# A column-gated layer's token sort with bf16 one-hots, weights placed later, gathers 12 tiles ahead and more unread matrix products

## The chip, the cores and the metric

The kernel runs on one core of a Trainium2 chip. A core has five engines that run their own instruction streams and wait for each other by semaphores: TensorE (PE in the profile; PEld is its loading of the stationary operand), VectorE (DVE), ScalarE (ACT), GpSimd (POOL) and SyncE (SP). Here SyncE and GpSimd issue the DMAs. TensorE's clock has two levels, 1.2 and 2.4 GHz; the profile shows what was granted as a share of 2.4 GHz. The metric is the device time of one execution in microseconds, as the median of several.

## The reference, cut to what matters

Four layers follow each other on 32 batches of 112 tokens with 256 features. Three of them (a depooling layer, a generated feed-forward layer and an attention layer) are not touched. The last one sends every token through one of 16 columns:

```python
def _L1_ffn_ref(x, col_emb, gate_w1, gate_b1, gate_w2, gate_b2, W_cols, b_cols, proj_w, proj_b, ln_g, ln_b):
    similarity = jnp.einsum('bsd,cd->bsc', _l2norm(x), _l2norm(col_emb))
    h = jax.nn.gelu(x @ gate_w1 + gate_b1, approximate=False)
    logits = similarity + jax.nn.sigmoid(h @ gate_w2 + gate_b2)
    _, top_idx = jax.lax.top_k(logits, 1)                   # one column of 16 for each token
    mask = jnp.sum(jax.nn.one_hot(top_idx, 16), axis=-2)
    weights = mask * jax.nn.softmax(logits, axis=-1)
    cols = jax.nn.gelu(jnp.einsum('bsd,cdn->bscn', x, W_cols) + b_cols, approximate=False)
    y = (cols * weights[..., None]).reshape(Bq, Sq, -1) @ proj_w + proj_b + x
    mu, var = jnp.mean(y, -1, keepdims=True), jnp.var(y, -1, keepdims=True)
    return (y - mu) * jax.lax.rsqrt(var + 1e-05) * ln_g + ln_b

x = x + jnp.tanh(g_ffn[1]) * _L1_ffn_ref(_layernorm(x), ...)
```

Since the mask leaves one column per token, only that column's product (256 to 64 features and back to 256) has to be computed.

## The kernel before

The kernel has a stage for each layer; the change is in `stage4` (from line 1497), the last one. It has two halves.

**Scoring and sort.** For groups of four batches TensorE turns the normalised tokens, computes the gate's products and the similarities, and ScalarE and VectorE make logits. VectorE then marks each token's best column (`hit`), counts along batches (`cum`), and TensorE's three products (lines 1987 to 1989) give each token's rank in its column. From the rank VectorE computes a slot. Slots are laid out by column in sub-tiles of 64, two to a tile of 128, 36 tiles in all (`N_TILES`), so a tile holds tokens of at most two columns. To invert the map, VectorE writes `in_tile` (which of 36 tiles, a one-hot, line 1856), `carry` (that one-hot times the token's number plus one, and times its weight, line 1861) and `spot` (which of 128 rows in the tile, in four quarters of eight batches, line 1865), all f32. TensorE multiplies `spot` of each of the 32 batches by `carry` and accumulates (line 1997): the result has, for each row and tile, the token's number and its weight. From it VectorE makes `comes_from`, `weight` and `goes_to` (lines 1870 to 1873) and then the columns of the 72 sub-tiles, `column_of` (lines 1875 to 1878).

Between these steps TensorE runs products that nobody reads: `busy(count, cols)` (line 1981) multiplies bf16 ones by a bf16 mask of 512 columns, or of `cols`, into PSUM bank 7.

**The tile loop.** For each of 36 tiles SyncE loads `column_of` twice into a register and issues two weight loads into a ring of four (lines 1633, 1634). GpSimd gathers the tile's rows by an indirect DMA (`fetch`, line 1666) and scatters finished rows (`store`, line 1674); its stream is written as `AHEAD4` = 5 gathers first, then for each n a gather n + 5 and the stores that are due after tile n. The first store is due after n = 5, so 11 gathers stand ahead of it. TensorE's stream for tile n is: `turn(n+1)` (two 128-column transposes, line 2006), `column(n)` (four products, 2017), `output(n-1)` (two register loads, 2022, and two products, 2026), and one unread product of 256 columns. ScalarE evacuates the turned rows (1725) and applies the gelu (1735), with a square root for every group of four tiles (1742). VectorE adds, takes statistics and finishes rows two tiles or more behind (1883 to 1910).

Every order here is written out by hand: each engine runs its list as it stands, and the waits between engines are semaphore counts. The unread products stand in TensorE's list, in front of what comes after them.

Of the kernel before, what the change touches and what calls it, by code (L numbers as in the profile page):

```python
# [19 lines left out]
ALU = mybir.AluOpType  # L20
# [3 lines left out]
BF16 = mybir.dt.bfloat16  # L24
I32 = mybir.dt.int32

B, T, D = 32, 112, 256
S2, DC = 375, 512
P = 128
# [892 lines left out]
def stage4_inputs(w):  # L922

    sb = lambda n, s, d=F32: w.ctx.enter_context(w.nc.sbuf_tensor(n, s, d))
    w.columns = {"col_emb": sb("s4_col_emb", [C4, D]), "cgate1": sb("s4_cgate1", [P, KD, P]),
                 "cgate1_b": sb("s4_cgate1_b", [P, 1]), "cgate2": sb("s4_cgate2", [P, C4]),
                 "cgate2_b": sb("s4_cgate2_b", [T, C4]), "w_cols": sb("s4_w_cols", [P, C4, KD * N4]),
                 "b_cols": sb("s4_b_cols", [N4, C4]), "proj": sb("s4_proj", [N4, F4 // N4 * D]),
                 "proj_b": sb("s4_proj_b", [T, D]), "proj_b_c": sb("s4_proj_b_c", [P, KD]),
                 "ln_g": sb("s4_ln_g", [P, D]), "ln_b": sb("s4_ln_b", [T, D]),  # L930
                 "col_less": sb("s4_col_less", [P, C4]), "steps": sb("s4_steps", [P, P + 1]),
                 "token": sb("s4_token", [T, B])}
    w.columns_in = w.sem("columns_in")
# [568 lines left out]
def stage4(w):  # L1502
# [6 lines left out]
    N_TILES, AHEAD4, SQRT_LAG = SLOT_TILES, 5, 2  # L1509
# [5 lines left out]
    with ExitStack() as ctx:  # L1515
# [30 lines left out]
        in_tile = sb("s4_in_tile", [T, B, N_TILES])  # L1546
        carry = sb("s4_carry", [T, B, 2, N_TILES])
        spot = sb("s4_spot", [T, B, P])
        pad = sb("s4_pad", [P, N_TILES])
        goes_to = sb("s4_goes_to", [P, N_TILES], I32)  # L1550
# [17 lines left out]
                 "counting", "cum_done", "rank_ps", "carry_done", "spot_done", "table_ps", "slots_done",  # L1568
# [12 lines left out]
        def wait(eng, name, count):  # L1581

            if count > 0:
                eng.wait_ge(S[name], count)
# [28 lines left out]
        with nc.Block() as block:  # L1613
# [26 lines left out]
            def _(pool):  # L1640
# [38 lines left out]
                wait(pool, "slots_done", 1)  # L1679
# [77 lines left out]
            def _(dve):  # L1757
# [102 lines left out]
                for part, of in enumerate((token, total)):  # L1860
                    nc.vector.tensor_tensor(carry[:, :, part, :], in_tile[:], of[:].unsqueeze(2).broadcast_to([T, B, N_TILES]),  # L1861
                                            ALU.mult).then_inc(S["carry_done"], 1)
                for q in range(4):
                    at = slice(q * 8, q * 8 + 8)
                    nc.vector.tensor_tensor(spot[:, at, :], steps[0:T, 0:P].unsqueeze(1).broadcast_to([T, 8, P]),
                                            within[:, at].unsqueeze(2).broadcast_to([T, 8, P]), ALU.is_equal)\
                        .then_inc(S["spot_done"], 1)
                wait(dve, "table_ps", 1)
                got = w.bank(1)[:, 2 * C4:2 * C4 + 2 * N_TILES].rearrange("p (k n) -> p k n", k=2)
                chain.link(nc.vector.tensor_scalar(pad[:], got[:, 0, :], 0.5, 65537.0, ALU.is_lt, ALU.mult))  # L1870
                nc.vector.tensor_scalar(comes_from[:], got[:, 0, :], -1.0, 0.0, ALU.add, ALU.max)
# [7 lines left out]
                wait(dve, "slots_done", 1)  # L1879
# [53 lines left out]
            def _(pe):  # L1933
# [51 lines left out]
                busy(24)  # L1985
# [6 lines left out]
                busy(36)  # L1992
                wait(pe, "carry_done", 2)
                for b in range(B):
                    if b % 8 == 0:
                        wait(pe, "spot_done", b // 8 + 1)
                    last = nc.tensor.matmul(w.bank(1)[:, 2 * C4:2 * C4 + 2 * N_TILES], spot[:, b, :],  # L1997
                                            carry[:, b, :, :].rearrange("t k n -> t (k n)"),
                                            start=(b == 0), stop=(b == B - 1))
                last.then_inc(S["table_ps"], 1)  # L2000

# [31 lines left out]
                turn(0)  # L2033
                for n in range(N_TILES):
# [5 lines left out]
                    busy(1, 256)  # L2040
# [3 lines left out]
def lay_out(x, ctx_2048, mask_BxS2_if0, g_xattn, g_ffn, L0_xattn_W_in, L0_xattn_b_in, L0_xattn_g_res,  # L2044
# [66 lines left out]
    out["token"] = (np.arange(B)[None] * T + np.arange(T)[:, None] + 1).astype(f32)  # L2111
# [14 lines left out]
```

## Time and profile before

| | us |
|---|---|
| median of 3 runs | 1323.33 (1322.43 to 1325.54) |
| the profiled execution, its own time | 1325.58 |
| its span, first to last instruction | 1323.6 |
| TensorE busy (matrix products) | 1227.8 (93%) |
| TensorE loading weights | 888.1 (67%) |
| VectorE busy | 958.7 (72%) |
| ScalarE busy | 676.3 (51%) |
| GpSimd busy | 583.4 (44%) |

The fourth stage runs from about 1080 us to the end: the scoring to about 1130, the sort to about 1168, the tile loop to about 1306.
### The profile page before, as it was taken

Reading aid. Unit: us, or ns where it says so; the run is one execution under the profiler, and the core shown is the slowest. Engines: PE = TensorE matmul, PEld = TensorE weight load, DVE = VectorE, ACT = ScalarE, POOL = GpSimd, SP = SyncE. Lnnn points to the kernel's source line nnn. Section 1 sums busy time; section 2 is a strip of 40 time slices with the busy share of each in tenths; the row PEclk is TensorE's granted clock in tenths of the full one; section 3 lists DMA queues with packets and bytes.
Section 4 is the critical chain, followed back from the end, with each engine's and each line's share of the span. In section 5 each row is a group of like instructions: output and inputs, shape, how many; then the busy total and the mean of one; then the engine's idle time right before and its main releaser. Section 6 shows DMA issues by size and latency. Waiting matters only on the chain. (4 is left out here: it accounts for less than half of the span.)

```text
span 1323.6 us, 33070 instructions
## 1 busy us (share of the span) xinstructions
PE 1227.8 (93%) x12491; PEld 888.1 (67%) x12491; DVE 958.7 (72%) x1666; ACT 676.3 (51%) x1497; POOL 583.4 (44%) x835
## 2 busy tenths in 40 slices
PE   4789999999999998699999999999999979889995
PEld 4565678778877885367667676767676657656663
DVE  7777665675576568788888888888888758624555
ACT  5845212202211222577888888788877653125442
POOL 1427888888875002633333333333333108034553
PEclk9999899999999999599999999999999988865555
DMA  8505445455453203976665666666666205243441
GB/s 222 144 4 192 139 132 166 137 152 154 146 154 97 72 1 50 159 114 96 97 99 95 96 95 95 96 95 95 95 95 95 37 1 160 64 124 108 141 134 38
DMA packets 111752, 141.80 MB, mean 107 GB/s; under 512 B 10317, under 2 KB 94776, under 8 KB 109380
## 3 DMA queue, kind: packets, MB, share of 16 engines
q1 hardware_dynamic: 97796, 96.14, 36.9%
q0 software_dynamic: 13824, 43.84, 11.3%
q8 instruction: 89, 1.46, 0.5%
q14 instruction: 43, 0.35, 0.1%
HBM read 105.79 MB, written 30.49 MB: 103 GB/s over the span
## 5 line engine op out<-in xcount | busy, mean ns | idle before, releaser
L1269 DVE TENSOR_REDUCE s_neg_max<-banks 112x3 bf16<-112x1461 f32 (+1 forms) x192 | 290.3, 1512 | 45.5 <-PE banks L1385 45.3
L1183 ACT ACTIVATE s_prob<-banks 128x448 f32<-128x448 f32 x512 | 272.6, 545 | 92.2 <-PE banks L1411 77.2
L714 DVE TENSOR_TENSOR s_m<-banks,s_base 128x512 f32<-128x512 f32 x256 | 161.1, 682 | 99.7 <-PE banks L868 99.4
L1411 PE MATMUL banks<-s_q_t,s_k_t 112*128 112x112 bf16 x2048 | 186.7, 215 | 1.1 <-ACT s_prob L1183 1.0
L1411 PEld LDWEIGHTS banks<-s_q_t,s_k_t 112*128 112x128 bf16 x2048 | 124.4, 98 | 72.7 <-issue 50.9
L868 PE MATMUL banks<-s_gate_sel,s_tw 64*128 64x256 f32 x1024 | 131.3, 396 | 1.2 <-DVE s_m L714 1.0
L911 PE MATMUL banks<-s_m,s_act_t 128*112 128x256 f32 x512 | 128.2, 388 | 1.5
L1427 PE MATMUL banks<-s_prob,s_v 128*32 128x112 f32 (+1 forms) x4096 | 126.3, 263 | 0.8 <-ACT s_prob L1183 0.7
L893 PEld LDWEIGHTS banks<-s_x_t,s_m 128*128 128x128 f32 x1024 | 116.7, 192 | 10.6 <-issue 7.6
L893 PE MATMUL banks<-s_x_t,s_m 128*128 128x112 f32 x1024 | 122.4, 278 | 0.0
L808 ACT ACT_TABLE_LOAD x8 | 10.3, 1283 | 205.3 <-PE banks L893 205.3
L868 PEld LDWEIGHTS banks<-s_gate_sel,s_tw 64*128 64x128 f32 x1024 | 95.2, 190 | 27.0 <-issue 9.7
L733 DVE SCALAR_TENSOR_TENSOR x_res<-banks,gates,x_res 112x512 f32<-112x512 f32 x128 | 93.0, 745 | 24.4 <-PE banks L911 21.0
L808 ACT ACTIVATE s_act_t<-banks,s_bias 128x112 f32<-128x112 f32 x256 | 68.9, 359 | 80.4 <-PE banks L893 80.3
L911 PEld LDWEIGHTS banks<-s_m,s_act_t 128*112 128x112 f32 x512 | 81.8, 176 | 38.7 <-issue 19.7
L1427 PEld LDWEIGHTS banks<-s_prob,s_v 128*32 128x32 f32 (+1 forms) x4096 | 94.9, 110 | 12.9 <-ACT s_prob L1183 1.0
L1067 POOL CAST s_qk<-s_rest 112x512 bf16<-112x512 f32 x32 | 19.6, 614 | 172.3 <-DVE s_rest L1258 172.3
L1057 POOL COPY s_v<-s_v_raw 128x768 f32<-128x768 f32 x32 | 26.3, 822 | 155.0 <-PE banks L1427 155.0
L1385 PE MATMUL banks<-s_k_t,s_q_t 32*112 32x487 bf16 x192 | 79.9, 416 | 5.7 <-DVE s_neg_max L1269 3.9
L1367 PE MATMUL banks<-s_ident,s_qk 112*128 112x112 bf16 x1024 | 73.4, 216 | 9.3 <-DVE s_q_t L1282 6.4
L1385 PE MATMUL banks<-s_k_t,s_q_odd 32*112 32x487 bf16 x320 | 80.4, 417 | 0.0
L2026 PE MATMUL banks<-s_proj,s_hid_c 64*128 x144 | 74.6, 671 | 0.7 <-ACT s_hid_c L1735 0.7
(304 smaller groups left out, 2284.7 us busy)
## 6 DMA issues: line engine op xcount, KB each, us to landing
k_parts<-s_k_split POOLq DMA_DIRECT2D x64, 281.2 KB, 3.5
s_k_t<-k_parts SPq DMA_DIRECT2D x32, 562.5 KB, 8.1
s_tw<-in_tw SPq DMA_DIRECT2D x16, 1024.0 KB, 5.1
s_k_raw<-in_ctx_k POOLq DMA_DIRECT2D x64, 187.5 KB, 3.6
s_k_t<-k_parts SPq DMA_DIRECT2D x32, 375.0 KB, 5.4
s_v_raw<-in_ctx SPq DMA_DIRECT2D x32, 256.0 KB
s_src<-in_ctx SPq DMA_DIRECT2D x8, 896.0 KB, 15.4
s_k_t<-k_parts SPq DMA_DIRECT2D x32, 187.5 KB, 9.2
```

The lines of the kernel that those rows point to most:

```text
L714: nc.vector.tensor_tensor(dst[:, :, :, rows_], got, base[:, :, rows_].unsqueeze(2).broadcast_to([P, 2, B, HR]), ALU.add).then_inc(S["merge ...
L733: nc.vector.scalar_tensor_tensor(out=w.x_res[:, 2 * p:2 * p + 2, :], in0=w.bank(6 + p % 2, T).rearrange("t (b d) -> t b d", b=2), scalar=w ...
L808: last = nc.scalar.activation(act_t[:, b, :], w.bank(4 + g % 2)[:, r * T:(r + 1) * T], ACT.Gelu_apprx_tanh, bias=bias1[:, c, b, :])
L868: last = nc.tensor.matmul(w.bank(2 * (n[1] % 2) + half)[:, m * B * HR:(m + 1) * B * HR], rows_(m)[tile], sel[tile], start=True, stop=True)
L893: last = nc.tensor.matmul(w.bank(4 + g % 2)[:, r * T:(r + 1) * T], m1[:, kk, b, :], x_t[:, kk, b * T:(b + 1) * T], start=(kk == 0), stop=( ...
L911: last = nc.tensor.matmul(y, act_t[:, b, :], m2[:, b, :], start=not first, stop=True)
L1183: nc.scalar.activation(prob[t % 2][:, c, :], w.bank(SCORE + n % SRING, P, TILE), ACT.Exp, scale=DH ** -0.5).then_inc(S["exp_done"], 1)
L1269: nc.vector.tensor_reduce(neg_max[half][:, ROWS + first:ROWS + end, 0], w.banks[0:T, MAX:MAX + end - first, 0:NKEY], AX.X, ALU.max, negate ...
L1385: last = nc.tensor.matmul(w.bank(MAX + place, T, NKEY), q, k_t[k][at, h, FIRST:FIRST + NKEY], start=True, stop=True)
L1411: last = nc.tensor.matmul(w.bank(SCORE + n % SRING)[:, s * T:(s + 1) * T], k_t[k][0:ROWS_MAX, h, c * P:(c + 1) * P], q_t[k][0:ROWS_MAX, h, :],
L1427: last = nc.tensor.matmul(w.banks[s * SLOT:(s + 1) * SLOT, OUT, t * T:(t + 1) * T], v[k][0:K_OF[c], c, t * HS + s, :], prob[t % 2][0:K_OF[ ...
L2026: last = nc.tensor.matmul(w.bank(4 + n % 3, P, D), hid_c[n % 2][:, k, :], proj[:, bass.ds(c * D, D)], start=(k == 0), stop=(k == 1))
```

## The change

The one-hots and carries become bf16, which a matrix product takes in one record instead of two. So that the token's number survives in bf16, it is carried in two parts, the batch (0 to 31) and the token in the batch plus one (1 to 112), and put together after the product (batch x 112 + token - 1). The weight is split into three bf16 parts and is placed by a product of its own, after the column numbers, into bank 6; `weight` is the sum of the three. The unread products of the sort are 32, 44, three pairs and 32 instead of 24, 36 and 16, and the tile loop runs two of 512 columns per tile instead of one of 256. TensorE waits for the weight placement ahead of `output(2)`, which writes bank 6. Gathers run 12 tiles ahead instead of 5. The diff, cut to its core:

```diff
@@ stage4
-    N_TILES, AHEAD4, SQRT_LAG = SLOT_TILES, 5, 2
+    N_TILES, AHEAD4, SQRT_LAG = SLOT_TILES, 12, 2
...
-        in_tile = sb("s4_in_tile", [T, B, N_TILES])
-        carry = sb("s4_carry", [T, B, 2, N_TILES])
-        spot = sb("s4_spot", [T, B, P])
+        in_tile = sb("s4_in_tile", [T, B, N_TILES], BF16)
+        carry = sb("s4_carry", [T, 5, B, N_TILES], BF16)
+        spot = sb("s4_spot", [T, B, P], BF16)
+        w_parts = sb("s4_w_parts", [T, 3, B], BF16)
+        rest = sb("s4_rest", [T, B])
...
@@ GpSimd
-                wait(pool, "slots_done", 1)
+                wait(pool, "slots_done", 2)
@@ VectorE
-                for part, of in enumerate((token, total)):
-                    nc.vector.tensor_tensor(carry[:, :, part, :], in_tile[:], of[:].unsqueeze(2).broadcast_to([T, B, N_TILES]),
-                                            ALU.mult).then_inc(S["carry_done"], 1)
+                nc.vector.tensor_scalar(carry[:, 0, :, :], in_tile[:], token[:, B:B + 1], None, ALU.mult)
+                nc.vector.tensor_tensor(carry[:, 1, :, :], in_tile[:], token[:, 0:B].unsqueeze(2).broadcast_to([T, B, N_TILES]),
+                                        ALU.mult).then_inc(S["carry_done"], 1)
...
+                chain.link(nc.vector.tensor_copy(w_parts[:, 0, :], total[:]))
+                chain.link(nc.vector.tensor_tensor(rest[:], total[:], w_parts[:, 0, :], ALU.subtract))
+                chain.link(nc.vector.tensor_copy(w_parts[:, 1, :], rest[:]))
+                chain.link(nc.vector.tensor_tensor(w_parts[:, 2, :], rest[:], w_parts[:, 1, :], ALU.subtract))
                 wait(dve, "table_ps", 1)
...
-                chain.link(nc.vector.tensor_scalar(pad[:], got[:, 0, :], 0.5, 65537.0, ALU.is_lt, ALU.mult))
-                nc.vector.tensor_scalar(comes_from[:], got[:, 0, :], -1.0, 0.0, ALU.add, ALU.max)
-                nc.vector.tensor_copy(weight[:], got[:, 1, :])
-                nc.vector.scalar_tensor_tensor(out=goes_to[:], in0=got[:, 0, :], scalar=-1.0, in1=pad[:],
-                                               op0=ALU.add, op1=ALU.add).then_inc(S["slots_done"], 1)
+                nc.vector.tensor_scalar(pad[:], got[:, 0, :], 0.5, 65537.0, ALU.is_lt, ALU.mult)
+                chain.link(nc.vector.tensor_scalar(found[:], got[:, 1, :], float(T), -1.0, ALU.mult, ALU.add))
+                chain.link(nc.vector.tensor_tensor(found[:], found[:], got[:, 0, :], ALU.add))
+                nc.vector.tensor_scalar(comes_from[:], found[:], 0.0, None, ALU.max).then_inc(S["slots_done"], 1)
+                nc.vector.tensor_tensor(goes_to[:], found[:], pad[:], ALU.add).then_inc(S["slots_done"], 1)
...
-                wait(dve, "slots_done", 1)
+                for part in range(3):
+                    nc.vector.tensor_tensor(carry[:, 2 + part, :, :], in_tile[:],
+                                            w_parts[:, part, :].unsqueeze(2).broadcast_to([T, B, N_TILES]), ALU.mult)\
+                        .then_inc(S["shares_done"], 1)
+                wait(dve, "shares_ps", 1)
+                got = w.bank(6, P, 3 * N_TILES).rearrange("p (k n) -> p k n", k=3)
+                chain.link(nc.vector.tensor_copy(weight[:], got[:, 2, :]))
+                for part in (1, 0):
+                    chain.link(nc.vector.tensor_tensor(weight[:], weight[:], got[:, part, :], ALU.add))
+                dve.sem_inc(S["weight_done"], 1)
@@ TensorE
-                busy(24)
+                busy(32)
...
-                busy(36)
-                wait(pe, "carry_done", 2)
+                busy(44)
+                wait(pe, "carry_done", 1)
                 for b in range(B):
                     if b % 8 == 0:
                         wait(pe, "spot_done", b // 8 + 1)
...
+                    last = placed(found_ps, slice(0, 2), b)
+                    if b % 8 == 7 and b < B - 1:
+                        busy(2)
                 last.then_inc(S["table_ps"], 1)
+                busy(32)
+                wait(pe, "shares_done", 3)
+                for b in range(B):
+                    last = placed(w.bank(6, P, 3 * N_TILES).rearrange("p (k n) -> p k n", k=3), slice(2, 5), b)
+                last.then_inc(S["shares_ps"], 1)
...
+                    if n == 2:
+                        wait(pe, "weight_done", 1)
...
-                wait(pe, "slots_done", 1)
-                busy(16)
                 wait(pe, "columns_done", 1)
+                wait(pe, "slots_done", 2)
...
-                    busy(1, 256)
+                    busy(2)
```

`placed(bank, parts, b)` is the product of `spot` of batch b with those parts of `carry`. Three places of the engines' lists show what moved.

TensorE, from the last unread products of the ranks to the first column products; `s_keep,s_ones` are the unread products, `s_carry,s_spot` the one-hot products, `ident,s_xn` the turns, `s_x_tt,s_w_tile` the column products. Before:

```order
L1981 MATMUL banks<-s_keep,s_ones 128x512 x36
L1997 MATMUL banks<-s_carry,s_spot 128x72 x32
L1981 MATMUL banks<-s_keep,s_ones 128x512 x16
L2006 MATMUL banks<-ident,s_xn 128x128 x4
L2017 MATMUL banks<-s_x_tt,s_w_tile 64x64 x4
L1981 MATMUL banks<-s_keep,s_ones 128x256
L2006 MATMUL banks<-ident,s_xn 128x128 x2
L2017 MATMUL banks<-s_x_tt,s_w_tile 64x64 x4
```

The same place after:

```order
L1997 MATMUL banks<-s_keep,s_ones 128x512 x44
L2010 MATMUL banks<-s_carry,s_spot 128x72 x8
L1997 MATMUL banks<-s_keep,s_ones 128x512 x2
L2010 MATMUL banks<-s_carry,s_spot 128x72 x8
...
L1997 MATMUL banks<-s_keep,s_ones 128x512 x32
L2010 MATMUL banks<-s_carry,s_spot 128x108 x32
L2033 MATMUL banks<-ident,s_xn 128x128 x4
L2044 MATMUL banks<-s_x_tt,s_w_tile 64x64 x4
L1997 MATMUL banks<-s_keep,s_ones 128x512 x2
L2033 MATMUL banks<-ident,s_xn 128x128 x2
L2044 MATMUL banks<-s_x_tt,s_w_tile 64x64 x4
```

The 32 one-hot products are cut into quarters with unread pairs between them, and a second set of 32 with 108 columns, behind 32 unread ones, stands ahead of the first turns.

VectorE, from the spot one-hots to the first row of the tile loop. Before:

```order
L1865 TENSOR_TENSOR s_spot<-s_steps,s_within 112x1024 x4
L1870 TENSOR_SCALAR s_pad<-banks 128x36
L1871 TENSOR_SCALAR s_comes_from<-banks 128x36
L1872 COPY s_weight<-banks 128x36
L1873 SCALAR_TENSOR_TENSOR s_goes_to<-banks,s_pad 128x36
L1875 TENSOR_TENSOR s_past<-s_steps,s_ends 1x1152
L1877 TENSOR_REDUCE s_column_f<-s_past 1x72
L1878 TENSOR_SCALAR s_column_of<-s_column_f 1x72
L1883 SCALAR_TENSOR_TENSOR s_xn<-banks,s_weight,s_xn 128x256
```

After, from the end of the weight's splitting:

```order
L1874 TENSOR_TENSOR s_w_parts<-s_rest,s_w_parts 112x32
L1877 TENSOR_SCALAR s_pad<-banks 128x36
L1878 TENSOR_SCALAR s_found<-banks 128x36
L1879 TENSOR_TENSOR s_found<-s_found,banks 128x36
L1880 TENSOR_SCALAR s_comes_from<-s_found 128x36
L1881 TENSOR_TENSOR s_goes_to<-s_found,s_pad 128x36
L1882 TENSOR_TENSOR s_past<-s_steps,s_ends 1x1152
L1884 TENSOR_REDUCE s_column_f<-s_past 1x72
L1885 TENSOR_SCALAR s_column_of<-s_column_f 1x72
L1887 TENSOR_TENSOR s_carry<-s_in_tile,s_w_parts 112x1152 x3
L1892 COPY s_weight<-banks 128x36
L1894 TENSOR_TENSOR s_weight<-s_weight,banks 128x36 x2
```

The weight's carry products and its sum now stand behind the column numbers, and four small operations (lines 1871 to 1874) stand ahead of the table.

GpSimd, the head of the tile loop. Before:

```order
L1666 DMA s_xn<-x_rows,s_comes_from 128x512 x11
L1674 DMA out_x<-s_xn,s_goes_to 3584x256
L1666 DMA s_xn<-x_rows,s_comes_from 128x512
L1674 DMA out_x<-s_xn,s_goes_to 3584x256
L1666 DMA s_xn<-x_rows,s_comes_from 128x512
```

After:

```order
L1669 DMA s_xn<-x_rows,s_comes_from 128x512 x16
L1669 DMA x_res<-x_rows,s_comes_from 128x512 x2
L1677 DMA out_x<-s_xn,s_goes_to 3584x256
L1669 DMA x_res<-x_rows,s_comes_from 128x512
L1677 DMA out_x<-s_xn,s_goes_to 3584x256
```

Eighteen gathers instead of eleven stand ahead of the first store; the ring's second half lies in the residual's buffer.

## Rows read from the trace of the kernel before

**Rows 1.** Stretches (us): length, busy time PE PEld DVE ACT POOL, clock, DMA share, GB/s.

```profile
1134.00:1138.00 4.00, 1.58 (x9) 0.59 (x7) 3.90 (x5) 1.61 (x3) 0.00 (x0) 1.00 0.00 1
1146.00:1149.50 3.50, 1.25 (x11) 1.13 (x11) 3.50 (x4) 0.00 (x0) 0.00 (x0) 1.00 0.00 0
1161.90:1166.60 4.70, 4.68 (x12) 1.66 (x13) 2.74 (x3) 0.00 (x0) 3.25 (x3) 0.50 0.30 76
1169.50:1173.50 4.00, 1.27 (x14) 1.02 (x15) 0.00 (x0) 1.02 (x4) 3.09 (x4) 1.00 0.88 260
...
1200.00:1220.00 20.00, 20.00 (x82) 13.24 (x82) 10.41 (x34) 8.79 (x25) 10.90 (x11) 0.50 0.46 133
```

**Rows 2.** Timeline, TensorE, sort and first tiles: start, us, what, [idle before <-releaser].

```profile
1138.22 7.93 PE L1981 MATMUL banks<-s_keep,s_ones 112*128 112x512 bf16 x36
1148.40 12.80 PE L1997 MATMUL banks<-s_carry,s_spot 112*128 112x72 f32 x64 [2.25 <-DVE s_spot L1865]
...
1170.65 0.65 PE L2017 MATMUL banks<-s_x_tt,s_w_tile 128*64 128x64 f32 x8 [2.12 <-DMA s_w_tile<-s_w_cols]
1171.23 0.28 PE L1981 MATMUL banks<-s_keep,s_ones 112*128 112x256 bf16 x1
1171.35 0.39 PE L2006 MATMUL banks<-ident,s_xn 128*128 128x128 f32 x2
...
1175.01 2.06 PE L2026 MATMUL banks<-s_proj,s_hid_c 64*128 x4 [0.75 <-ACT s_hid_c L1735]
```

**Rows 3.** Timeline, TensorE, one tile of the loop.

```profile
1199.81 0.39 PE L1981 MATMUL banks<-s_keep,s_ones 112*128 112x256 bf16 x1
...
1200.00 0.63 PE L2006 MATMUL banks<-ident,s_xn 128*128 128x128 f32 x2
...
1200.56 1.12 PE L2017 MATMUL banks<-s_x_tt,s_w_tile 128*64 128x64 f32 x8
...
1201.60 2.07 PE L2026 MATMUL banks<-s_proj,s_hid_c 64*128 x4
...
1203.61 0.39 PE L1981 MATMUL banks<-s_keep,s_ones 112*128 112x256 bf16 x1
```

**Rows 4.** Timeline, VectorE, the sort's one-hots and what follows the table.

```profile
1144.49 1.36 DVE L1861 TENSOR_TENSOR s_carry<-s_in_tile,s_token 112x1152 f32<-112x1152 f32 x1
...
1147.04 4.62 DVE L1865 TENSOR_TENSOR s_spot<-s_steps,s_within 112x1024 f32<-112x1024 f32 x4
1161.24 0.20 DVE L1870 TENSOR_SCALAR s_pad<-banks 128x36 f32<-128x36 f32 x1 [9.57 <-PE banks L1997]
...
1164.53 0.18 DVE L1878 TENSOR_SCALAR s_column_of<-s_column_f 1x72 int32<-1x72 f32 x1
```

**Rows 5.** Chain of waits at the loop's start: start, us, what it spent them on.

```profile
1168.20 0.49 SPq L1634
...
1169.38 3.81 DMA s_w_tile<-s_w_cols
```

**Rows 6.** Source view of the weight loads, line 1634, all 72.

```profile
DMA to landing us min/median/max: 1.8/1.9/4.3
```

**Rows 7.** Timeline, GpSimd, a store and the gather behind it.

```profile
1202.35 1.01 POOL L1674 DMA_INDIRECT out_x<-s_xn,s_goes_to  x1 [1.38 <-DVE s_xn L1910]
1203.66 0.98 POOL L1666 DMA_INDIRECT s_xn<-x_rows,s_comes_from  x1 [0.30 <-issue]
```

**Rows 8.** Timeline, TensorE, attention stage: eight bf16 products with 128 weight columns.

```profile
700.52 0.56 PE L1367 MATMUL banks<-s_ident,s_qk 112*128 112x112 bf16 x8
```

**Rows 9.** Timeline, ScalarE, evacuation of the first two turned tiles.

```profile
1168.20 1.14 ACT L1725 ACTIVATE s_x_tt<-banks,s_neg_b 128x128 f32<-128x128 f32 x4 [32.55 <-PE banks L2006]
```

**Rows 10.** Chain of waits, end of the loop and tail.

```profile
1302.80 1.05 PE banks L2017 x8
...
1305.89 0.48 DVE s_xn L1883
...
1315.84 1.58 POOLq L1613
```

More of the change, by code:

```diff
@@ L931, in stage4_inputs @@
                  "col_less": sb("s4_col_less", [P, C4]), "steps": sb("s4_steps", [P, P + 1]),
-                 "token": sb("s4_token", [T, B])}
+                 "token": sb("s4_token", [T, B + 1])}
     w.columns_in = w.sem("columns_in")
@@ L1545, in stage4 @@
         pos, tile_of, within = (sb("s4_" + n, [T, B]) for n in ("pos", "tile_of", "within"))
-        in_tile = sb("s4_in_tile", [T, B, N_TILES])
-        carry = sb("s4_carry", [T, B, 2, N_TILES])
-        spot = sb("s4_spot", [T, B, P])
+        in_tile = sb("s4_in_tile", [T, B, N_TILES], BF16)
[3 more added lines that the diff above has]
+        rest = sb("s4_rest", [T, B])
         pad = sb("s4_pad", [P, N_TILES])
+        found = sb("s4_found", [P, N_TILES])
         goes_to = sb("s4_goes_to", [P, N_TILES], I32)
@@ L1567, in stage4 @@
                  "col_ss_done", "col_n_done", "col_t_ps", "col_t_done", "biased", "kept", "x_biased", "kept_late", "x_biased_late",
-                 "counting", "cum_done", "rank_ps", "carry_done", "spot_done", "table_ps", "slots_done",
+                 "counting", "cum_done", "rank_ps", "carry_done", "spot_done", "table_ps", "slots_done", "shares_done", "shares_ps", "weight_done",
                  "columns_done", "turned", "x_tt_done", "col_ps", "gelu_done", "y_ps", "summed", "stat_done",
@@ L1990, in _, with placed @@
                                  stop=True).then_inc(S["rank_ps"], 1)
-                busy(36)
-                wait(pe, "carry_done", 2)
+                def placed(bank, parts, b):
+                    return nc.tensor.matmul(bank, spot[:, b, :], carry[:, parts, b, :],
+                                            start=(b == 0), stop=(b == B - 1))
+                busy(44)
+                wait(pe, "carry_done", 1)
+                found_ps = w.bank(1)[:, 2 * C4:2 * C4 + 2 * N_TILES].rearrange("p (k n) -> p k n", k=2)
                 for b in range(B):
@@ L1996, in _ @@
                         wait(pe, "spot_done", b // 8 + 1)
-                    last = nc.tensor.matmul(w.bank(1)[:, 2 * C4:2 * C4 + 2 * N_TILES], spot[:, b, :],
-                                            carry[:, b, :, :].rearrange("t k n -> t (k n)"),
-                                            start=(b == 0), stop=(b == B - 1))
+                    last = placed(found_ps, slice(0, 2), b)
+                    if b % 8 == 7 and b < B - 1:
+                        busy(2)
                 last.then_inc(S["table_ps"], 1)
+                busy(32)
[3 more added lines that the diff above has]
+                last.then_inc(S["shares_ps"], 1)
                 def turn(n):
@@ L2110, in lay_out @@
     out["steps"] = np.concatenate([np.tile(np.arange(P), (P, 1)), np.arange(P)[:, None]], 1).astype(f32)
-    out["token"] = (np.arange(B)[None] * T + np.arange(T)[:, None] + 1).astype(f32)
+    out["token"] = np.concatenate([np.tile(np.arange(B), (T, 1)), np.arange(T)[:, None] + 1], 1).astype(f32)
     return {k: np.ascontiguousarray(v) for k, v in out.items()}
```

## Prediction

> **What bounds the kernel now.** I read the slices of the page first: TensorE's granted clock reads 0.8 or 0.9 through most of the span and 0.5 in the last four, the part that the change rewrites. Then the stretches [rows 1], the timelines of TensorE, VectorE and GpSimd, the chain of waits and the weight-load line of the source view. The last stage ends in a loop over 36 gathered tiles. In it TensorE is busy for 20.00 of 20.00 us, at a granted clock of 0.50 (1.2 of 2.4 GHz), while VectorE has 10.41, ScalarE 8.79 and GpSimd 10.90 us [rows 1]. One tile takes 3.80 us from one unread product to the next, 1199.81 to 1203.61, and its parts fill it: unread product 0.19, two turns 0.56, column products 1.04, output products 2.01 [rows 3]. So the loop is bound by TensorE at its lower level.
>
> How it got there: ahead of the loop the 64 one-hot records take 12.80 us [rows 2], 0.20 each. They begin in a stretch in which TensorE was busy 1.25 of 3.50 us, behind which the clock fell. Sixteen unread products (4.68 of 4.70 us busy at 0.50) brought it back; then TensorE waited for weights, 1.27 of 4.00 us busy, and it fell for good. A stretch with 1.58 of 4.00 us busy did not lose it [rows 1]. The loop at 20.00 of 20.00 never got it back: busy time in a record is not what decides.
>
> **The sort.** VectorE's last quarter of the spot one-hots ends at 1147.04 + 4.62 = 1151.66, and the table is read at 1161.24 [rows 4]; in between stand the f32 products. With bf16 operands a product is one record. The nearest row is eight bf16 products with 128 weight columns in 0.56 us, 0.07 each [rows 8]. The last eight stand behind the last quarter, so the table is ready at about 1152.3: 8.9 us earlier. The four small operations that split the weight cost about 0.20 each, as the table's first row does [rows 4]; 0.8 us, of which those eight products hide 0.6. The decoding has one more dependent step of 0.2. Together -8.45 us: the column numbers, done at 1164.71 before (1164.53 + 0.18), are done at 1156.3. Bounds: the first of the two carry operations now has a per-partition scalar instead of a broadcast operand; it may cost the old 1.36 or a good deal less, so up to 1 us can be gained. The unread pairs between quarters (0.44) fit beside a quarter of 1.16.
>
> **The weights later.** Three carry products of 1.36 [rows 4] come behind the column numbers: 4.1 us, to 1160.4. The 32 unread products there (0.22 each, 7.93 / 36 [rows 2], 7.0 us) run from 1152.3 to 1159.3 and cover most of it, leaving about 1 us idle. Then 32 products of 108 columns, 0.07 each: 2.2 us, to 1162.6. The wait for shares_done has the gathered rows' turns queued behind it on TensorE. Two turns (0.39 for the pair [rows 2]) and the first evacuation (1.14 for two rows [rows 9]) put the first column product near 1163.7, against 1170.65: 7 us earlier. Its weights don't hold it: they land 5.9 us after the column numbers now (1164.71 to 1170.65), so at 1162.2. weight_done is due at about 1163.3, far ahead of the third output product that waits for it.
>
> The eight small products and the 32 are where a rule speaks against the trace. The row of eight gives 0.07 each [rows 8]. The Trainium skill, "TensorE: Matmul & The Clock Gate", LDWEIGHTS, states a load of P / 1.2 ns for P columns, 107 ns for 128; by that the 32 would take 3.4 us instead of 2.2 and the kernel would come out 1.2 us later. The same page's section on the weight path allows faster loads for bf16 with 128 columns, and the row agrees with that.
>
> **The tile at full clock.** Column products 0.58 (1170.65 to 1171.23 [rows 2]); output products half of 2.01 and turns half of 0.56 [rows 3], so 1.00 and 0.28, estimates; two unread products 0.44. Sum 2.30 us against 3.80. Then something else is late. SyncE issues two weight loads a tile, one each 1.18 us when nothing holds it (1168.20 to 1169.38 [rows 5]): 2.36 us, 2.4 with a little for its wait. GpSimd needs 1.31 for a store and 1.28 for a gather [rows 7], 2.6 a tile while it does both, but with gathers 12 tiles ahead 18 of the 36 stand before the first store (11 now), and from there, about the sixth tile (1179), the other 18 gathers and 36 stores are 18 x 1.28 + 36 x 1.31 = 70 us: done near 1249, not after the loop. VectorE has 10.41 us in 5.26 tiles, 2.0 each, and ScalarE 1.7 [rows 1]. I take SyncE's 2.4. The tail from the last output to the end, 1323.6 - 1305.89 = 17.7 us [rows 10], is VectorE, stores and their drain and stays.
>
> Sum: 1163.7 + 35 x 2.4 = 1247.7; last tile's products 2.3; 2 us for weights that land late while the 18 gathers run (below); tail 17.7. Span 1269.7 instead of 1323.6. The profiled execution took 1325.58, 2.0 more than its span, and lies 2.25 above the median, so the median is forecast at 1269.7 + 2.0 - 2.25 = **1269 us**. Its own range: 1263 (2.36 us a tile, the shorter carry, no late weights) to 1284 (2.8 us a tile).
>
> **Rival 1: the clock is lost as the loop starts, and the kernel is slower.** Place: between the turn of tile 1 and the first output product. There TensorE waits for the evacuation, then for the second tile's weights (now 8.5 us behind the column numbers, 1169.38 + 3.81 against 1164.71 [rows 5], so at 1164.8), then for ScalarE and its own two register loads before the output (landed at 1173.19, output at 1175.01: 1.8 us [rows 2, 5]). In about 4.1 us it has 0.58 + 0.44 + 0.2 + 0.58 = 1.8 us of work. Ahead of the two falls it had 1.25 of 3.50 and 1.27 of 4.00; with 1.58 of 4.00 it kept the clock [rows 1]. This is nearer to the last, but not by much. If it falls, the loop gives nothing back: a half-clock tile now has two products of twice 0.2 instead of one of 0.2, so 3.78 (132.15 / 35, 1170.65 to 1302.80 [rows 2, 10]) + 0.6 = 4.4 us, and 35 of them with the last tile's 3.1 and the tail end at 1163.7 + 153.3 + 3.1 + 17.7 = 1337.8: a median of **1337 us**. For it: 20 of 20 us busy at half clock did not raise it [rows 1]. Against it: the gap of 1169.5 to 1173.5 had no unread pair and no third turn.
>
> **Rival 2: lost in mid-loop.** Each tile at half clock costs 2.0 us more, so a fall after tile k gives 1269 + 2.0 x (36 - k); it decides for slower where k is under 9. Place: the square-root turns, where ScalarE's table loads hold an output. About 1296.
>
> **Rival 3: the clock holds but weights land late all along.** Gathers and weight loads share what moves them: 0.88 of the DMA engines were busy at 260 GB/s while gathers ran [rows 1], and loads landed in 3.81 there and at most 4.3, against a median of 1.9 [rows 5, 6]. The first two tiles' weights landed 2.65 us apart. 18 gathers of 1.28 make 23 us, 9 tiles at 0.25: the 2 us above. If it lasted for the whole loop, 35 x 0.25 = 9 instead of 2: **1276 us**. The Trainium skill, "DMA: Bandwidth & Descriptors", Issuing engines are not separate DMA queues, says that DMAs of all issuing engines run on the same 16 engines and interleave. By that rule gathers further ahead push weights back; the trace agrees for the first tiles.
>
> **How the numbers follow.** Forecast (clock held, 2.4 to 2.6 us a tile) 0.50; rival 3 0.10; rival 1 0.28; rival 2 0.12, of which a third is slower. Within 0.2%, about what a measurement can tell from no change, lies only a narrow strip of rival 2: 0.01. Faster 0.50 + 0.10 + 0.07 = 0.67, slower 0.32. Leaving rival 1 out would leave out more than 2 in 10, so the range is 1263 to 1339, though little is expected in its middle; the forecast's own is 1263 to 1284.
>
> **What would show it.** Right: granted clock 1.00 from 1138 to the last tile, one-hot products under 1 us a quarter, the column numbers near 1156, tiles 2.4 to 2.6 us apart with SyncE's loads back to back. Wrong: 0.50 in the loop with tiles 4.4 us apart; or full clock with tiles at 2.8 or more, and then the wait on TensorE ahead of the column products (weights) or the output (ScalarE) says whose it is.

## The result, and the profile after

The changed kernel takes 1278.2 us (median of 4 executions, 1276.39 to 1280.07) against 1324.43 before; the ratio is 0.964, 95% interval 0.960 to 0.968. The forecast was 1269 us with a range of 1263 to 1339: the kernel is faster by the mechanism that was named, and by 9 us less. The profiled execution took 1278.38 us with a span of 1276.6. In five of the kernels below the range ends between 1310 and 1350 us; those executions had a lower mean granted clock than their siblings (0.905 to 0.936 instead of 0.957 to 0.968), the ratios leave them out, and the medians and ranges count them.

The page's slices after, TensorE's busy tenths and its granted clock in tenths of 2.4 GHz:

```profile
PE   4798899999999999589999999999999996998994
PEclk9998899999999999779999999999999999889997
```

The 0.5 of the last four slices is gone: from the sort on, the clock falls only behind the last product. (Ahead of the sort both traces have short falls.) Two stretches of the loop (columns as in [rows 1]):

```profile
1180.00:1200.00 20.00, 19.30 (x129) 12.70 (x127) 14.28 (x48) 14.07 (x38) 12.79 (x14) 1.00 0.67 197
1200.00:1220.00 20.00, 19.05 (x127) 12.70 (x127) 15.64 (x52) 13.76 (x37) 15.42 (x16) 1.00 0.69 200
```

Against the last of [rows 1] TensorE is again the fullest engine, but at 1.00, and no longer quite full. VectorE's timeline through the sort, which answers to [rows 4]:

```profile
1149.57 0.52 DVE L1863 TENSOR_SCALAR s_carry<-s_in_tile,s_token 112x1152 bf16<-112x1152 bf16 x1
...
1151.27 4.62 DVE L1868 TENSOR_TENSOR s_spot<-s_steps,s_within 112x1024 bf16<-112x1024 f32 x4
...
1156.69 0.20 DVE L1877 TENSOR_SCALAR s_pad<-banks 128x36 f32<-128x36 f32 x1
...
1160.20 0.18 DVE L1885 TENSOR_SCALAR s_column_of<-s_column_f 1x72 int32<-1x72 f32 x1
1160.31 3.88 DVE L1887 TENSOR_TENSOR s_carry<-s_in_tile,s_w_parts 112x1152 bf16<-112x1152 bf16 x3
```

TensorE's timeline over the loop's start, which answers to [rows 2]; the bracket is idle time ahead:

```profile
1164.24 1.69 PE L2010 MATMUL banks<-s_carry,s_spot 112*128 112x108 bf16 x32 [0.95 <-DVE s_carry L1887]
1165.77 0.61 PE L2033 MATMUL banks<-ident,s_xn 128*128 128x128 f32 x4
1166.94 0.68 PE L2044 MATMUL banks<-s_x_tt,s_w_tile 128*64 128x64 f32 x8 [0.56 <-ACT s_x_tt L1728]
...
1169.63 1.12 PE L2055 MATMUL banks<-s_proj,s_hid_c 64*128 x4 [0.64 <-issue]
...
1173.08 1.12 PE L2055 MATMUL banks<-s_proj,s_hid_c 64*128 x4 [0.79 <-issue]
```

The profile puts the idle time ahead of these outputs down to "issue". The source view of TensorE's sequencer, the part that hands it its instructions, shows more. Here are its one wait between 1170 and 1171.5 us (it starts at 1169.9; min/median/max in ns) and its reads of the two column numbers behind it:

```profile
L1587 PEldq EVENT_SEMAPHORE  x1: 1657/1657/1657, 1169.9 to 1169.9; - x1
L2049 PEldq TENSOR_LOAD <-s_column_of x2: 305/314/324, 1171.7 to 1172.3; - x2
```

The wait lasts from 1169.92 to 1171.58 us, and by the trace's semaphore records the last piece of the third tile's weights lands at 1171.54. Only then does the sequencer read the numbers, some 1.3 us with their checks, and the output at 1173.08 starts 0.79 us behind the column products. Five more such waits, 0.28 to 1.26 us long, each end 0.03 to 0.04 us behind a landing of weights, the last at 1184.45.

One tile in the chain of waits, where each piece reaches to the next (against [rows 3]):

```profile
1207.91 0.54 PE banks L1997 x2
1208.45 0.22 PE banks L2033 x2
1208.67 0.61 PE banks L2044 x8
1209.28 1.06 PE banks L2055 x4
1210.34 0.54 PE banks L1997 x2
```

A tile that waits for nothing takes 2.43 us. VectorE's sum behind the last output but one, which [rows 10] has at 1305.89:

```profile
1258.85 0.48 DVE L1899 SCALAR_TENSOR_TENSOR s_xn<-banks,s_weight,s_xn 128x256 f32<-128x256 f32 x1
```

**Where the 47.0 us of span went.** Four marks cut both spans: the first carry operation, the first column product, that sum, the end.

| | before | after | difference |
|---|---|---|---|
| up to the first carry | 1144.49 | 1149.57 | +5.1 |
| to the first column product | 26.16 | 17.37 | -8.8 |
| to the sum | 135.24 | 91.91 | -43.3 |
| to the end of the span | 17.7 | 17.75 | 0 |

The first row lies in the scoring. The only edit ahead of its end is eight more unread products in front of the ranks, and TensorE still waits 0.71 us for VectorE behind them (2.42 before), so they delay nothing. In the trace after, the granted clock is 0.50 from 1125 to 1129, in the scoring, where the trace before has 1.00. The mark moves by itself: e1, the same program up to there, has it at 1144.45, and over all traces below it stands anywhere from there to 1153.49. So kernels are compared by what follows the mark: 179.1 us before, 127.0 after.

### The profile page after: what moved, and what is told of

Its sections match the earlier page's. It is cut to its first block and busy times, and to the rows that moved or that the text cites. A ratio compares the mean times of both kernels' runs of the same rounds, so it can differ in the third digit from the quotient of the medians.

```text
span 1276.6 us, 33231 instructions
## 1 busy us (share of the span) xinstructions
PE 1180.1 (92%) x12565; PEld 852.2 (67%) x12565; DVE 963.9 (76%) x1677; ACT 674.7 (53%) x1497; POOL 587.9 (46%) x835
## 5 line engine op out<-in xcount | busy, mean ns | idle before, releaser
L1337 PE MATMUL banks<-s_wqk,s_x_t 128*112 128x512 f32 x128 | 70.9, 639 | 1.0 <-ACT s_x_t L1127 1.0
```

## The experiments

**Theory A**: gaps in the sort and at the loop's start decide the clock, and past them any tile keeps it. **Theory B**: the pair of unread products in each tile holds it. **Theory F**: what paces the tile is TensorE with the waits behind ScalarE's table loads. The last column counts from the mark.

| run | median (range, executions) | ratio to before (95%) | from the mark |
|---|---|---|---|
| e1 old unread product in the loop | 1317.47 (1313.57 to 1321.96, 7) | 0.994 (0.992 to 0.997) | 168.5 |
| e2 none in the loop | 1315.06 (1313.11 to 1315.87, 4) | 0.992 (0.989 to 0.995) | 163.9 |
| e10 one of 512 in the loop | 1325.34 (1323.03 to 1328.17, 10) | 1.000 (0.998 to 1.002) | 175.3 |
| e5 pair in eight tiles | 1304.06 (1300.16 to 1310.24, 4) | 0.982 (0.980 to 0.985) | 162.3 |
| e3 sort without fill | 1275.9 (1272.57 to 1341.55, 4) | 0.961 (0.957 to 0.965) | 128.5 |
| e4 before, with the pair | 1354.04 (1350.84 to 1354.68, 4) | 1.020 (1.017 to 1.024) | 199.8 |
| e6 before, gap filled, with the pair | 1290.98 (1285.67 to 1349.38, 4) | 0.972 (0.968 to 0.975) | 140.2 |
| e7 gathers 5 ahead | 1283.77 (1280.43 to 1310.21, 4) | 0.966 (0.963 to 0.969) | 130.8 |
| e8 no square root | 1272.84 (1270.58 to 1277.09, 4) | 0.960 (0.957 to 0.963) | 124.0 |
| e9 pair ahead of the output | 1277.84 (1275.13 to 1349.46, 6) | 0.964 (0.962 to 0.967) | 127.7 |
| e11 three edits | 1277.09 (1274.51 to 1349.6, 6) | 0.963 (0.960 to 0.966) | 128.0 |
| e12 roots of eight tiles | 1273.05 (1271.86 to 1277.16, 6) | 0.960 (0.957 to 0.963) | 126.0 |

### Less unread work in the loop

```diff
 e1                e2                e10
-busy(2)          -busy(2)          -busy(2)
+busy(1, 256)                       +busy(1)
```

> The changed kernel with the loop's old unread product (one of 256 columns per tile instead of two of 512). Theory A (the gaps of the sort and of the loop's start decide the clock; once past them any tile keeps it): granted clock 1.00 to the last tile. TensorE's tile falls from 2.42 us by 0.44 - 0.11 to 2.09, so something else sets the pace: SyncE's two weight loads, 2.36, or ScalarE's square-root turns. At 2.36 to 2.45 a tile instead of 2.557 over 35 tiles the time is 1278.2 - 4 to 7 = about 1273. Theory B (the pair of 512 columns in each tile holds the clock): the clock falls to 0.50 in the loop and a tile takes 3.80 as before, 35 x (3.80 - 2.56) = 43 us more: about 1321.

> The changed kernel with no unread product in the tile loop (those of the sort stay). Theory A: clock 1.00 in the whole loop; TensorE's tile would be 2.42 - 0.44 = 1.98, so the pace is that of SyncE (2.36) or of ScalarE, and the time is within 2 us of the run with one product of 256 columns, about 1272. Theory B: the clock falls soon after the loop's start and a tile takes 3.80 - 0.19 = 3.6: 35 x (3.6 - 2.56) = 36 us more, about 1315.

> The changed kernel with one unread product of 512 columns per tile instead of two. If half the pair is enough for the clock: 1.00 to the last tile, TensorE's tile 2.42 - 0.22 = 2.20, SyncE's 2.36 or ScalarE's turns set the pace, 35 x 0.06 to 0.1 = 2 to 4 us less: about 1275. If it is not enough (one of 256 was not): the clock falls somewhere in the loop, 4.0 us a tile from there (3.6 + 0.43), so 1290 if it falls half way and about 1328 if it falls at the start; I expect this one, with a place that differs from run to run.

All three lost the clock, with the sort as in the changed kernel. The stretches around the fall, of e1, e2 and e10 in turn:

```profile
1162.60:1166.50 3.90, 2.54 (x18) 1.62 (x17) 0.83 (x2) 1.95 (x8) 2.90 (x4) 1.00 0.86 250
1166.50:1170.50 4.00, 3.46 (x14) 2.47 (x15) 0.53 (x3) 0.70 (x3) 3.09 (x4) 0.50 0.90 272
```

```profile
1166.50:1170.40 3.90, 2.25 (x16) 1.41 (x14) 1.09 (x3) 1.67 (x7) 2.97 (x4) 1.00 0.92 268
1170.40:1174.40 4.00, 3.28 (x12) 2.12 (x13) 1.09 (x3) 0.99 (x4) 2.83 (x3) 0.50 0.92 261
```

```profile
1169.60:1173.10 3.50, 2.17 (x16) 1.39 (x15) 1.09 (x3) 1.13 (x4) 2.83 (x3) 1.00 0.86 263
1173.10:1177.00 3.90, 3.90 (x16) 2.47 (x16) 1.09 (x3) 1.13 (x4) 2.83 (x3) 0.50 0.88 257
```

In each it is the place of rival 1: the first two to four tiles, where TensorE waits for weights, ScalarE and its own register loads. In the changed kernel the same place reads

```profile
1167.50:1171.50 4.00, 3.36 (x23) 2.00 (x20) 0.67 (x2) 1.53 (x6) 2.87 (x4) 1.00 0.83 245
1171.50:1175.50 4.00, 3.09 (x26) 2.15 (x25) 1.52 (x5) 1.64 (x6) 2.99 (x4) 1.00 0.91 262
```

The pair makes the difference, and half of it is not enough: at 0.50 the single product of e10 only lengthens the tile (4.02 us instead of 3.67 in e2), back to the time of before. So the sort's fill alone does not carry the clock over the loop's start. Whether a tile further on keeps it without a pair, the second half of theory A, these runs don't show: they never got that far.

### The pair in the first eight tiles only

```diff
-                    busy(2)
+                    if n < 8:
+                        busy(2)
```

> The changed kernel with the unread pair in the first eight tiles only and none in the other 28. Theory C (the pair is needed only over the loop's start, where TensorE waits for weights, ScalarE and its register loads; a tile's own products hold a clock that is already high): clock 1.00 to the last tile, TensorE's part of a tile falls from 2.42 to 1.98 and SyncE's two loads (2.36) or ScalarE's square-root turns set the pace: 28 x 0.1 to 0.2 = 3 to 6 us less than the changed kernel, about 1273. Rival B (the pair holds the clock in every tile): the clock falls soon after the eighth tile, at a square-root turn, and a tile takes 3.6: 28 x (3.6 - 2.56) = 29 us more, about 1307.

All four executions lost it. In the profiled one it fell in the seventh tile, still with a pair:

```profile
1178.00:1182.00 4.00, 2.38 (x17) 1.46 (x17) 1.92 (x8) 3.71 (x7) 1.89 (x2) 0.99 0.87 276
1182.00:1186.00 4.00, 4.00 (x17) 2.34 (x16) 1.69 (x5) 1.21 (x5) 0.00 (x0) 0.50 0.30 90
```

That tile waited 0.62 us ahead of its column products and 1.00 ahead of the output, both put down to issue. The sequencer's wait ahead of it, in ns:

```profile
L1587 PEldq EVENT_SEMAPHORE  x1: 2185/2185/2185, 1177.8 to 1177.8; - x1
```

It ends at 1179.94, 0.03 us behind the last landing of that tile's weights: late weights, not a missing pair, stand ahead of this fall. The other three executions, 4 to 10 us shorter and with a higher mean clock (0.929 to 0.936 instead of 0.924), probably fell later, in tiles without the pair (there a tile costs 3.67 us at half clock and, by its parts, 2.0 to 2.4 at full); that is worked out, not seen. Theory C's 1273 came in no execution, but a fall for want of the pair behind the eighth tile isn't shown either, so whether the pair is needed in every tile stays open.

### The pair, and the fill, in the kernel before

```diff
 e4                       e6
-busy(1, 256)            -busy(1, 256)
+busy(2)                 +busy(2)
                         -busy(16)
                         +busy(32)
```

> The kernel before with only the loop's unread products changed: two of 512 columns per tile instead of one of 256. Theory A: the clock is lost ahead of the loop as before (gap behind the first column products) and the pair does not bring it back: 0.50 in the whole loop, a tile longer by 0.86 - 0.21 = 0.65 us, 36 x 0.65 = 23 us: about 1347, ratio to before 1.017. Theory B: the pair keeps the clock or brings it back, a tile takes 2.56, and the loop is 43 us shorter: about 1281.

> The kernel before with unread products alone changed: 32 instead of 16 ahead of the first turns, and two of 512 columns per tile instead of one of 256; one-hots stay f32, gathers stay 5 ahead. Theory D (the clock is all that the loop gained, and filling the gap ahead of it is enough): clock back at 1.00 by 1166 as before, kept over the loop's start, first column product some 2 us later than before (about 1172.7), then 2.56 us a tile: 1323.3 + 2 - 43 = about 1282, and what is left to the changed kernel is the earlier sort, about 8.8 us less 5 for its later scoring. Rival E (the wait for the second tile's weights behind the column numbers drops the clock, whatever stands ahead of it): 0.50 in the loop and 4.4 us a tile as in the run with the pair alone: about 1354.

e4 fell behind the first of these stretches, in the wait for the second tile's weights, and stayed down:

```profile
1175.90:1179.30 3.40, 1.41 (x12) 0.94 (x12) 0.00 (x0) 1.00 (x4) 2.75 (x3) 1.00 0.89 262
...
1200.00:1220.00 20.00, 20.00 (x70) 11.75 (x69) 7.68 (x26) 9.12 (x23) 5.97 (x6) 0.50 0.26 73
```

Its tiles are 4.44 us apart (1183.74 to 1188.18), the 4.4 of rival 1: here the pair does not bring back a lost clock, though TensorE is busy for 20.00 of 20.00 us. With the gap filled as well the old kernel got it back, kept it in three of four executions and gained 2.8%:

```profile
1170.40:1174.40 4.00, 4.00 (x20) 1.88 (x19) 0.00 (x0) 0.00 (x0) 2.83 (x3) 0.99 0.82 230
1174.40:1178.40 4.00, 3.20 (x28) 2.09 (x26) 0.00 (x0) 2.27 (x8) 3.05 (x4) 1.00 0.90 267
```

From the mark 179.1 became 140.2: 38.9 of the 52.1 us are unread products alone, and 13.2 are left for the earlier sort (8.8, and 1.7 that the fill delayed) and, by what remains, 2.7 for the gathers. Theory D had some 41 for the unread products. The fourth execution, 1349.38 at a mean clock of 0.906, is near rival E's 1354; it has no trace.

### The sort without its fill

```diff
-                    if b % 8 == 7 and b < B - 1:
-                        busy(2)
...
-                busy(32)
                 wait(pe, "shares_done", 3)
```

> The changed kernel without the unread pairs between the quarters of the one-hot products and without the 32 unread products ahead of the weight's placement; the pair in each tile stays. Theory A: TensorE waits for VectorE's one-hots and then for the weight's carries (0.56 us of products per 1.16 us, then some 4.5 us of nothing), the clock falls there and the loop does not bring it back: 4.4 us a tile, 35 x (4.4 - 2.56) = 64 us more, about 1340. Theory B (the pair decides): the pair brings the clock back within the first tiles, about 1278 to 1284.

```profile
1154.20:1159.90 5.70, 0.00 (x0) 0.00 (x0) 5.60 (x6) 0.00 (x0) 5.09 (x3) 0.50 0.40 115
1159.90:1164.20 4.30, 3.93 (x36) 3.53 (x36) 0.58 (x3) 0.67 (x3) 3.38 (x4) 0.50 0.60 158
1164.20:1168.00 3.80, 3.79 (x21) 2.75 (x22) 0.00 (x0) 1.65 (x7) 2.89 (x4) 0.52 0.89 262
1168.00:1172.00 4.00, 4.00 (x24) 2.43 (x23) 1.70 (x5) 1.59 (x6) 3.04 (x4) 1.00 0.86 266
```

The clock fell as expected, and came back at 1168: the 32 weight products, the turns and the first tile's products, drawn out by the half clock, left one gap of 0.35 us. One execution of four took 1341.55 at a mean clock of 0.905, which fits a loop at half clock; it has no trace. So where the return succeeds the fill is worth 1.5 us from the mark, and theory A's 1340 is the exception. Theory B's number came, though not by the pair alone: of the busy time ahead of the return the one pair in it took 1.03 us. Why 7.7 busy us there raised the clock and 20 full ones of e4 didn't stays open.

### What paces the tile

```diff
 e7
-    N_TILES, AHEAD4, SQRT_LAG = SLOT_TILES, 12, 2
+    N_TILES, AHEAD4, SQRT_LAG = SLOT_TILES, 5, 2
 e8
-nc.scalar.activation(y_root[:, at], y_var[:, at], ACT.Sqrt).then_inc(S["y_root_done"], 1)
+nc.scalar.activation(y_root[:, at], y_var[:, at], ACT.Identity).then_inc(S["y_root_done"], 1)
```

> The changed kernel with ScalarE's square root of the variances replaced by a plain copy, so that no function table is loaded in the tile loop (the rows come out wrongly scaled; all else is as it was). Theory F (the two table loads at each group's end hold one output per group by 0.34 to 0.61 us): those seven waits go, 3.3 us less, tiles all 2.42 apart behind the first eight, about 1275. Rival G (another engine, SyncE or GpSimd, holds the tiles at the same pace anyway): the waits come back at other places and the time stays at 1278.

> The changed kernel with gathers 5 tiles ahead as before instead of 12. If the gathers ahead carry nothing: time within 0.2% of the changed kernel, 1278 (1275 to 1281). If GpSimd becomes the bound, since it must store (1.32) and gather (1.29) in each tile from the sixth on, a tile takes at least 2.61 instead of 2.557 for some 25 tiles: 1 to 4 us more, 1279 to 1282, with TensorE waiting for gathered rows ahead of a turn. If 18 gathers in a row held the weights back at the start, the first eight tiles get shorter: up to 2 us less.

ScalarE's timeline of the changed kernel at a group's end, and TensorE's output that waits for it:

```profile
1202.29 0.51 ACT L1738 ACTIVATE s_hid_c<-banks,s_b_cols 64x64 f32<-64x64 f32 x2 [0.90 <-PE banks L2044]
1202.81 1.28 ACT L1745 ACT_TABLE_LOAD   x1
1204.11 0.21 ACT L1745 ACTIVATE s_y_root<-s_y_var 128x4 f32<-128x4 f32 x1
1204.22 0.61 ACT L1728 ACTIVATE s_x_tt<-banks,s_neg_b 128x128 f32<-128x128 f32 x2
1204.84 1.28 ACT L1738 ACT_TABLE_LOAD   x1
1206.14 0.51 ACT L1738 ACTIVATE s_hid_c<-banks,s_b_cols 64x64 f32<-64x64 f32 x2
```

```profile
1206.79 1.12 PE L2055 MATMUL banks<-s_proj,s_hid_c 64*128 x4 [0.61 <-ACT s_hid_c L1738]
```

Between two gelus 3.34 us pass, more than a tile. TensorE's waits in the loop, in the changed kernel and then in e8 (us in total, times, longest):

```profile
PE banks L2055 <- ACT s_hid_c L1738: 3.0, 6, 0.6
PE banks L2055 <- issue: 2.5, 5, 0.8
```

```profile
PE banks L2055 <- issue: 1.1, 3, 0.7
...
PE banks L2055 <- ACT s_hid_c L1738: 0.8, 1, 0.8
```

Six waits of the changed kernel are put down to ScalarE; a seventh at a group's end, 0.34 us at 1216.9, counts as issue, though the gelu that it needs ends only at 1216.75, behind a table load. Without the loads the waits at the groups' ends are gone (the 0.8 left in e8 stands at the loop's start, at 1170.8) and the time from the mark is 3.0 us shorter, against 3.3 expected: theory F. e7 took 3.8 us more from the mark, inside its 1 to 4 (5.6 by the medians), and one execution took 1310.21 at a mean clock of 0.936. GpSimd there issues almost without a pause from the first store to 1257:

```profile
1215.43 1.01 POOL L1677 DMA_INDIRECT out_x<-s_xn,s_goes_to  x1 [0.30 <-issue]
1216.75 0.98 POOL L1669 DMA_INDIRECT x_res<-x_rows,s_comes_from  x1 [0.30 <-issue]
1218.03 1.01 POOL L1677 DMA_INDIRECT out_x<-s_xn,s_goes_to  x1 [0.31 <-issue]
```

2.60 us for a gather and a store, more than the 2.43 of TensorE: with gathers 5 ahead GpSimd is the bound. TensorE's waits there read issue too (6.1 us, 14 times), but by the semaphore records a tile's rows land 0.04 to 1.1 us ahead of its turn from 1195 to 1250, and 12 to 21 us ahead in the changed kernel. The third clause of e7's text shows as well, if faintly: the first eight tiles are 0.4 us shorter (20.7 instead of 21.1).

### Three tries to take the waits away

```diff
 e9 (and e11)
                     column(n)
+                    busy(2)
                     if n >= 1:
                         output(n - 1)
-                    busy(2)
 e11, e12
-    ENDS = [4 * g + 3 for g in range((N_TILES - 4) // 4)] + [N_TILES - 3, N_TILES - 1]
+    ENDS = [7, 15, 23, 27, 31, N_TILES - 3, N_TILES - 1]
...
-                upto = min(ready, done + (2 if i >= N_TILES - 6 else 1))
+                upto = min(ready, done + (2 if i >= N_TILES - 8 else 1))
```

e11 also has the wait for the weight's carries and the weight's products behind `turn(0)` (not shown here).

> The changed kernel with the unread pair of each tile moved from behind the output products to in front of them, so that it stands where TensorE waits (for the gelu behind two table loads, and for its register loads in the first tiles). Theory F (these waits, 5.2 us in 11 places, are what the loop lost against 2.42 a tile): the pair's 0.44 covers most of each wait, 4 to 4.5 us less, and the waits of 0.3 to 0.6 ahead of the outputs are gone: about 1274. Rival G (the pair only pushes the outputs back, and VectorE or GpSimd behind them gives it back): 1278. Rival H (the clock falls, since nothing stands behind the output any more): 1300 or more.

> The changed kernel with the pair moved in front of the output products, the weight's placement moved behind the first tile's turns (so that their evacuation runs beside it), and square roots for groups of eight tiles in the first 24 instead of four. Expected: as the run with the moved pair (1274), less 1.0 us for the evacuation (0.56 idle and part of the turn) and up to 0.5 for three table-load turns whose waits the pair does not cover whole: about 1272.5. If rows of the first tile land later than 1164.2 of the changed kernel's trace, the weight's placement waits for them and the 1.0 is not gained.

> The changed kernel with square roots for groups of eight tiles in the first 24 (group ends 7, 15, 23, 27, 31, 33, 35 instead of 3, 7, 11, 15, 19, 23, 27, 31, 33, 35), rows finished two at a time from tile 28; unread products where the changed kernel has them. Theory F: three of the seven waits behind table loads (0.33 to 0.61 us, mean 0.48) go, 1.4 us less than the changed kernel: about 1277; in the trace four such waits are left, each at a group's end. Up to the loop's start the program is the changed kernel's word for word: if the clock can be lost there by chance of where a stretch begins, one or two of the executions come out near 1340 as in the runs before; if the changed kernel holds it safely, none does.

e9 has no wait of TensorE left between 1170 and 1255, and no gain. A tile in its chain of waits:

```profile
1198.91 0.37 PE banks L2033 x2
1199.28 0.61 PE banks L2044 x8
1199.89 0.54 PE banks L1997 x2
1200.42 1.06 PE banks L2055 x4
1201.48 0.26 PE banks L2033
```

The turns take 0.37 behind the output products and 0.22 behind the unread ones, so each tile is 0.15 us dearer, 35 x 0.15 = 5 us, what the waits had cost. G's number came, by another way than G's: the pair pays for 0.15 of its 0.54 where it stood. One execution of six took 1349.46 at a mean clock of 0.908, as H has it; it has no trace. e11 inherits the dearer tile. Its placement behind the turn brings the first column product to 16.53 us from the mark instead of 17.38, but the third tile's is no earlier than in e9 (22.28 and 22.25), and two of its six executions took 1342 and 1350 at mean clocks of 0.909 and 0.908. e12 leaves the pair in its place and loads tables less often. From its first to its last column product it takes 88.1 us instead of 89.5, the expected 1.4 less, and the expected four waits for ScalarE at groups' ends are left up to there (0.34 to 0.44 us); from the mark it is 1.0 us shorter. With 1273.05 us it is the fastest with its square roots in place, but most of the 5 us to the changed kernel's median lies ahead of the mark (1144.79 and 1149.57 in the profiled executions), and the intervals of the two ratios overlap. None of its six executions shows a low clock.

## Why the prediction came out as it did

- **The bound before, and the clock.** Right: full clock from the sort to the last product, the loop's 135.2 us down to 91.9.
- **The sort.** Right: -8.45 forecast, -9.4 measured: from the first carry to the column numbers 20.22 us before (1144.49 to 1164.71) and 10.81 now (1149.57 to 1160.38). Nearly all of the rest is the first carry operation, 0.52 instead of 1.36, the gain that the bounds allowed for.
- **The weights later.** From column numbers to the first column product 7.4 us forecast, 6.56 measured: the idle time was the expected 1 us (0.95), and the 32 products took 1.69 us instead of 2.2. The 3.4 us that the prediction set beside its sum did not come. The Trainium skill, "TensorE: Matmul & The Clock Gate", LDWEIGHTS, states P / 1.2 ns, 107 ns for a load of 128 columns; here the loads' own records last 97 ns on the mean, close to that, but they overlap and one product follows another every 0.05 us, so the loads don't add up.
- **The tile: the step that failed inside a right forecast.** 35 x 2.4, with SyncE as the bound, became 35 x 2.557 (1166.94 to the last column product at 1256.45, waits at the loop's start included). Two terms were mis-sized. TensorE's own tile is 2.43, not 2.30 (0.54, 0.22, 0.61 and 1.06 for 0.44, 0.28, 0.58 and 1.00), so SyncE never comes to bound. And ScalarE was costed by its mean, 1.7 us a tile, which spreads the two table loads of a group over four tiles; in the tile where they stand they hold an output, seven times 0.33 to 0.61, 3.3 us (e8, e12). Rival 2 had named that place for the clock, and not for time.
- **Late weights.** The 2 us were about right, by a way that the prediction did not have: weights held TensorE's sequencer up to 1184, and as it then still has to read two column numbers, the waits stand ahead of outputs (0.79, 0.57 and 0.20 us) and not of column products (0.12). These are 1.7 us; the 0.64 ahead of the first output has no late weights before it. Rival 3, weights late in the whole loop, did not occur.
- **The sum.** Of the 6.9 us between 1269.7 and 1276.6 the scoring has +5.1, which runs differ in anyway, the way to the first column product -1.8 and the loop +3.6. The median lies about another 1.9 above, mostly since the profiled execution after stands at its median and the one before stood 2.25 above its own. So part of the distance to 1269 is chance in the scoring and not a fault of the sum.
- **Rival 1** got its place right (e1, e2, e10), its tile (4.44 in e4) and nearly its time: 1337 forecast, 1341.55 to 1349.6 in executions of e3, e9 and e11 with a low mean clock (none of them traced). The change itself had none in four, nor e12 in six; with the pair's position, the sort's fill or the gathers changed some have, so its margin seems thin: that four of four held may in part be luck, and 0.28 was not too high a chance.
- **Rival 2** did not occur: the clock held at the square-root turns.

## What to carry to other kernels

Where a loop of short products runs at half clock, look for the gap in which the clock was lost, fill that, and keep unread work in the loop, at its start at least: in the loop the one without the other gave nothing or a loss (e1, e4), both gave 2.8% without any other edit (e6). Where dense work follows the gap by itself, as in the changed sort, the fill mattered little in three executions of four (e3). Once TensorE is twice as fast, cost every other engine by its worst tile and not by its mean. And where filler stands matters: it can be worth part of its own time to the instruction behind it (e9). A wait that the profile calls issue may have a cause one step earlier: look at what held the engine's sequencer before.

## What was not expected of the hardware

A loop that keeps TensorE busy for 20.00 of 20.00 us at 0.50 doesn't raise the clock even with two 512-column products in each tile (e4), while 7.7 us of dense products at the end of the sort did (e3). Two 128-column f32 turns take 0.22 us behind bf16 unread products and 0.37 behind f32 output products (e9); the runs show the price, and not its cause. Two register loads ahead of an output occupy TensorE's sequencer for about 1.3 us; where late weights held it first (1.66 us in the third tile), the wait shows ahead of the output and as "issue", not at the weights.
